# Two-layer conditioned feed-forward kernel: packed and split input loads, a reordered start of TensorE's work, and the last blocks written one tile earlier

## The reference, cut to what matters

```
W = L0_cond_weights[itok_B_0_15]                 # (128, 32, 32)
z = einsum('bct,bcd->bdt', x, W)
base = einsum('bsd,od->bso', z, W_base) + b_base
e0, e1 = z @ enc0.T, z @ enc1.T                  # ranks 32 and 8
w0, w1 = coefs0 * mask0, coefs1 * mask1          # 3 experts, (3, 512, 32) and (3, 512, 8)
decoded = einsum('bsr,eor->ebso', e0, w0) + einsum('bsr,eor->ebso', e1, w1)
update = real_fourier_orthogonal_multiply(decoded).sum(axis=0)   # fixed 512x512 orthogonal basis
x = x + base + 0.5 * update
y = einsum('bct,bcd->bdt', x, L1_cond_weights[itok_B_0_30])
x = x + scale * einsum('bsi,if->bsf', y, 2 * kernel - 1)
```

## Time and profile before

| what | before |
|---|---|
| median of three runs | 219.19 us |
| the profiled execution | 219.81 us, of which the span shown is 218.0 us |
| PE (matmul) | 213.1 us busy, 98% of the span |
| ACT | 125.2 us, 57% |
| DVE | 122.5 us, 56% |
| POOL | 111.6 us, 51% |
| one steady step of a tile on PE | 6.24 us |

### The profile page before, as it was taken

The page is one execution under the profiler, slowest core; times in us unless marked ns, Lnnn a source line. Parts: engine busy times, 40 slices in busy tenths (PEclk is TensorE's granted clock), DMA queues, the critical chain, the costliest instruction groups (busy, mean ns, idle before and its releaser), DMA issues.

```text
span 218.0 us, 4565 instructions
## 1 busy us (share of the span) xinstructions
PE 213.1 (98%) x1441; PEld 191.6 (88%) x1441; DVE 122.5 (56%) x216; ACT 125.2 (57%) x395; POOL 111.6 (51%) x133
## 2 busy tenths in 40 slices
PE   7999999999999999999999999999999999999985
PEld 2879999999999999999999999999999999999964
DVE  4676555545665554456655554566555455665443
ACT  2467765555666555556665555566655555666340
POOL 3677866655445666454446664554566645423100
PEclk9999999999999999999999999999999999999999
DMA  6991054433334444423244444333444432331112
GB/s 181 327 355 60 9 155 155 147 117 118 123 102 148 150 149 148 134 74 142 103 150 150 148 149 131 83 134 106 150 150 147 150 120 97 125 109 48 50 48 96
DMA packets 18042, 28.58 MB, mean 131 GB/s; under 512 B 3146, under 2 KB 5066, under 8 KB 18034
## 3 DMA queue, kind: packets, MB, share of 16 engines
q1 hardware_dynamic: 15360, 26.73, 36.4%
q0 software_dynamic: 2048, 1.05, 2.3%
q10 hardware_dynamic: 626, 0.70, 1.1%
HBM read 20.09 MB, written 8.39 MB: 131 GB/s over the span
## 4 chain that ended last, share of the span: by engine, by line
PE 96%; ACT 1%; DVE 1%; issue 0%
PE z_ps L565 41%; PE a_ps L608 13%; PE f_ps L619 13%; PE f_ps L615 13%; PE f_ps L597 7%; PE f_ps L600 3%; PE f_ps L512 2%; PE a_ps L518 1%; ACT blocks L311 0%; PE a_ps L619 0%; PE a_ps L615 0%; PE z_ps L512 0%; DVE a_low L465 0%; PE a_ps L546 0%; ACT a_high L347 0%
## 5 line engine op out<-in xcount | busy, mean ns | idle before, releaser
L235 POOL DMA_INDIRECT gathered<-in_L_cond_weights,row_now x56 | 54.6, 975 | 13.0 <-issue 8.9
L448 DVE TENSOR_TENSOR y_low<-a_ps,y_high 128x512 fp32r<-128x512 f32 x32 | 22.1, 692 | 67.2 <-ACT y_high L330 67.2
L330 ACT ACTIVATE y_high<-a_ps 128x512 fp32r<-128x512 f32 x32 | 19.2, 599 | 70.0 <-PE a_ps L608 70.0
L565 PE MATMUL z_ps<-a_high,xt_high 128*128 128x256 f32 x256 | 50.6, 279 | 0.2 <-DVE a_low L465 0.2
L565 PE MATMUL z_ps<-a_low,xt_high 128*128 128x256 f32 x256 | 50.4, 279 | 0.0
L242 POOL TENSOR_TENSOR x<-x_in,bias 128x512 f32<-128x512 f32 x32 | 40.9, 1280 | 14.9 <-DVE xt_low L407 11.0
L565 PE MATMUL z_ps<-a_high,xt_low 128*128 128x256 f32 x256 | 47.7, 289 | 0.0
L565 PEld LDWEIGHTS z_ps<-a_high,xt_high 128*128 128x128 f32 x256 | 41.1, 188 | 3.1 <-issue 0.5
L565 PEld LDWEIGHTS z_ps<-a_low,xt_high 128*128 128x128 f32 x256 | 38.9, 188 | 0.0
L565 PEld LDWEIGHTS z_ps<-a_high,xt_low 128*128 128x128 f32 x256 | 36.7, 190 | 0.1
L311 ACT ACTIVATE blocks<-mix_parts 32x64 fp32r<-32x64 f32 x128 | 32.6, 255 | 3.1
(11 more groups left out here) (66 smaller groups left out, 180.3 us busy)
## 6 DMA issues: line engine op xcount, KB each, us to landing
x_in<-in_x SPq DMA_DIRECT2D x32, 256.0 KB, 3.0
xt_in<-in_x_t SPq DMA_DIRECT2D x31, 256.0 KB, 2.7
out_x<-x SPq DMA_DIRECT2D x31, 256.0 KB, 2.0
gathered<-in_L_cond_weights,row_now POOLq DMA_INDIRECT x56, 2.5
w_sb<-in_L_ffn_W_base SPq DMA_DIRECT2D x3, 256.0 KB, 6.6
basis_sb<-in_fourier_basis SPq DMA_DIRECT2D x1, 258.0 KB, 3.7
w_sb<-in_L_ffn_W_base ACTq DMA_DIRECT2D x1, 256.0 KB, 6.6
xt_in<-in_x_t ACTq DMA_DIRECT2D x1, 256.0 KB
```

What stands on the lines that cost most here:

```text
L235: nc.gpsimd.indirect_dma_start(gathered[:, slot, layer, :], None, mix_rows[layer], IndirectOffsetOnAxis(rows[:, layer:layer + 1].bitcast(u ...
L448: nc.vector.tensor_tensor(out=y_low[:, slot % PAIR, :], in0=y_ps[slot % PAIR][:, :], in1=y_high[:, slot % PAIR, :].bitcast(f32), op=ALU.su ...
L565: last = nc.tensor.matmul(z_ps[slot % PAIR][:, columns], xt[:, slot % PAIR, k * P:(k + 1) * P], a[:, k, columns], start=(start and half == ...
```

## The change

It has five parts.

1. Coefficients, masks and kinds become one array `packed`, 664 words on each of 128 rows (480 of coefficients, 120 of masks, 64 of kinds). SP's queue loads rows 0 to 63 of it and of the basis, ACT's queue rows 64 to 127 (`load_side`). One semaphore for both halves.
2. SP's queue then loads W blocks 0 and 1 and both xt tiles 0 and 1, ACT's queue enc and W blocks 2 and 3.
3. 10 instead of 13 matmuls on zeros at the start, none between the transposes, and the transposes go in the order 0, 2, 1, 3.
4. `low_sum` uses all 128 rows of `enc_parts` and `spectrum_low` (which adds the product of two low parts), and follows `high_sum` bank by bank. Tile 0 is multiplied by A as its parts come (`feed0_first`), high parts first, each low part one block later.
5. In the step of tile 28, ACT and DVE also split tile 31's mix matrices, and ACT writes their blocks, after those of tile 30; the step of tile 29 has no blocks left to write.

The core of the diff:

```diff
+        def load_side(queue, rows):
+            queue.dma_start(packed[rows, :], packed_in[rows, :]).then_inc(packed_loaded, 16)
+            queue.dma_start(basis_sb[rows, :, :], basis[rows, :, :]).then_inc(basis_loaded, 16)
         def _(sp):
-            sp.dma_start(coefs_sb[:, :, :, :], coefs).then_inc(coefs_loaded, 16)
-            sp.dma_start(basis_sb[:, :, :], basis).then_inc(basis_loaded, 16)
-            for c in range(CHUNKS - 1):
-                load_w(sp, c)
+            load_side(sp, slice(0, ENC_LOW))
+            load_w(sp, 0)
+            load_w(sp, 1)
+            sp.dma_start(xt_in[:, 0, :], xt_tiles[0]).then_inc(xt_loaded[0], 16)
             sp.dma_start(xt_in[:, 1, :], xt_tiles[1]).then_inc(xt_loaded[1], 16)
         def _(act):
-            act.dma_start(masks_sb[:, :, :, :], masks).then_inc(masks_loaded, 16)
-            act.dma_start(kinds[:, :, :], kinds_in).then_inc(kinds_loaded, 16)
+            load_side(act, slice(ENC_LOW, P))
             act.wait_ge(enc_zero, 1)
             act.dma_start(enc_sb[0:R, :], enc).then_inc(enc_loaded, 16)
-            load_w(act, CHUNKS - 1)
-            act.dma_start(xt_in[:, 0, :], xt_tiles[0]).then_inc(xt_loaded[0], 16)
+            load_w(act, 2)
+            load_w(act, 3)
...
+            def feed0_first():
+                pe.wait_ge(xt_low_ready, 1)
+                for k in range(CHUNKS):
+                    pe.wait_ge(a_high_ready, k + 1)
+                    feed0_part(0, xt_high, a_high, k, start=(k == 0))
+                    feed0_part(0, xt_low, a_high, k)
+                    if k >= 1:
+                        pe.wait_ge(a_low_ready, k)
+                        feed0_part(0, xt_high, a_low, k - 1)
+                pe.wait_ge(a_low_ready, CHUNKS)
+                feed0_part(0, xt_high, a_low, CHUNKS - 1, stop=True).then_inc(fed0, 1)
...
```

More of the change, by code:

```diff
@@ L358, in _, with step @@
             expand0(1, 1)
-            def step(tile, u, turn, early=False, new=True):
+            def step(tile, u, turn, early=False, last=False, new=True):
                 high_y(tile, u, recycled=not early or u >= PAIR)
-                split_mix((u + 2) % RING, turn + (u + 2) // RING)
+                if new:
+                    split_mix((u + 2) % RING, turn + (u + 2) // RING)
+                if last:
+                    split_mix((u + 3) % RING, turn + (u + 3) // RING)
                 if new:
@@ L365, in step @@
                 high_z(tile + 2, (u + 2) % RING)
-                expand1((u + 2) % RING, tile + 2, recycled=not early or u >= 2)
-                expand0((u + 2) % RING, tile + 2)
+                if new:
+                    expand1((u + 2) % RING, tile + 2, recycled=not early or u >= 2)
+                    expand0((u + 2) % RING, tile + 2)
+                if last:
+                    expand1((u + 3) % RING, tile + 3)
+                    expand0((u + 3) % RING, tile + 3)
             for u in range(RING):
@@ L373, in _ @@
                     step(turn * RING + u, u, turn)
-            step(TILES - 4, 0, TURNS - 1)
+            step(TILES - 4, 0, TURNS - 1, last=True)
             step(TILES - 3, 1, TURNS - 1, new=False)
@@ L476, in _, with step @@
             dve.wait_ge(scale_loaded, 16)
-            def step(tile, u, early=False):
+            def step(tile, u, early=False, last=False):
                 low_y(tile, u, recycled=not early or u >= PAIR)
                 low_mix(tile + 2, (u + 2) % RING)
+                if last:
+                    low_mix(tile + 3, (u + 3) % RING)
                 low_xt(tile + 3, (u + 3) % RING)
@@ L657, in _ @@
                 feed1(TILES - 1, 3, end_ps[half], halves[half])
-INPUTS = ["x", "x_t", "kinds", "L0_cond_weights", "L0_ffn_W_base", "L0_ffn_b_base", "enc", "coefs", "masks",
+INPUTS = ["x", "x_t", "packed", "L0_cond_weights", "L0_ffn_W_base", "L0_ffn_b_base", "enc",
           "L1_cond_weights", "L1_ffn_kernel", "L1_ffn_scale"]
@@ L681 @@
     inputs["x_t"] = np.asarray(inputs["x"]).reshape(TILES, P, CHUNKS, P).transpose(0, 3, 2, 1).reshape(TILES, P, T)
-    inputs["kinds"] = kinds_by_partition(inputs["itok_B_0_15"], inputs["itok_B_0_30"])
+    kinds = kinds_by_partition(inputs["itok_B_0_15"], inputs["itok_B_0_30"])
     inputs["enc"] = np.concatenate([inputs["L0_ffn_enc0"], inputs["L0_ffn_enc1"]])
-    inputs["coefs"] = by_partition(inputs["L0_ffn_coefs0"], inputs["L0_ffn_coefs1"])
-    inputs["masks"] = by_partition(inputs["L0_ffn_mask0"], inputs["L0_ffn_mask1"])
+    parts = (by_partition(inputs["L0_ffn_coefs0"], inputs["L0_ffn_coefs1"]),
+             by_partition(inputs["L0_ffn_mask0"], inputs["L0_ffn_mask1"]), kinds)
+    inputs["packed"] = np.concatenate([np.ascontiguousarray(part).reshape(P, -1).view(np.int32) for part in parts], axis=1)
     arrays = {name: np.ascontiguousarray(inputs[name]) for name in INPUTS}
```

58 lines of the change are left out of this document (24 added, 34 removed).

## The result

| | before | after |
|---|---|---|
| median (range) of six runs each, us | 219.15 (218.78 to 219.70) | 217.76 (217.55 to 218.38) |
| ratio, 95% interval | | 0.9934 [0.9915, 0.9953] |
| profiled execution, its span | 219.81, 218.0 | 217.55, 215.7 |

The change makes the kernel 1.4 us faster, inside the range given (215.5 to 218.0) and 1.2 us short of the 216.6 forecast. Span against span it is 2.3 us, near the 2.55 of the sum. The two differ because single executions scatter: 18 of the kernel before on another chip took 218.67 to 220.79. Its profiled one lay 0.66 above the median here, and the changed kernel's profiled one was the fastest of its six. What was slow in the first is worked out further down, under *The base*.

A forecast was written before the change was run, and what follows sets the result against it. PE, 96% of the span, bounds the kernel and only its two ends can pay: 1.6 us (start) plus 0.95 (end) takes 219.81 to 217.3; with the median 0.6 lower, the forecast is 216.6, range 215.5 to 218.0.

The forecast's parts named there:

- the sum: Whole kernel: 1.6 us from the start plus 0.95 from the end, 2.55 in all, off the profiled execution.
- The base: Starting point of the sum: the profiled execution of 219.81 us, with the median taken as 0.6 lower, at 219.19.
- Part 5: End, tile 31: PE's wait of 0.79 us for ACT's blocks goes; gain 0.95 us (0.8 to 1.1).
- Part 4: Start, ACT: waits for tile 0's second gather until 14.6, then 5.5 us; `mix1` at 20.1, 1.6 us earlier, not 2.6.
- Part 1: Start: basis matmuls begin at 6.25 instead of 6.47, gain 0.2 us (0 to 0.5); packed load costed at nothing.
- Part 2: Transposes and sums: fillers between transposes go, saving 0.88 us; bank 0 complete 1.65 earlier, `a_high` at 10.65.
- Rows cost nothing: Low sums: 128 rows instead of 64 take no longer, three sums 0.89 against 0.87 us, row-count changes included.
- Part 3: Tile 0's feed: only two matmuls follow the last `a_low`; tile 1's feed starts at 14.15 instead of 16.73, 2.6 earlier.
- Rival (a): Start: the gathers land sooner, so the gain is 3.55 us, time 215.6; chance 0.17.
- Rival (b): Start: TensorE's clock rises only after the basis matmuls, which take 1.8 us longer; time 217.4; chance 0.14.
- Rival (c): Start: the packed load lands 1 us later, gain 0.6 + 0.95, time 217.6; chance 0.09 together with another rival.
- Rival (d): Start: clock stays at 1.2 GHz up to tile 0's feed; 3.2 us slower, 222.4; chance 0.05.

The follow-up runs named there:

- change, again: The changed kernel unaltered, run once more beside its variants on one chip: ratio 0.9928 to the kernel before, 218.16 us.
- 13 fillers: The changed kernel with 13 instead of 10 matmuls on zeros at the start: ratio 0.9922 to the kernel before, 218.00 us.
- loads as before: The changed kernel with parts 1 and 2 undone (separate loads, old queues), W transposed in order 0, 1, 3, 2: ratio 0.9892 to before, 217.14 us.
- the same, gathers ahead: Kernel of the row above, x tiles 1-3 and xt 3 issued after tile 0's matrices landed: 0.9857 (loads as before), 0.9851 (whole pieces), 0.9897 (basis whole).
- gathers ahead: The changed kernel with SP issuing x tiles 1 to 3 and xt tile 3 only after tile 0's matrices landed: ratio 0.9909 to before, 217.50 us.
- whole pieces: The changed kernel with packed loaded whole on SP's queue and the basis whole on ACT's queue: ratio 0.9907 to before, 217.79 us.
- basis whole: The changed kernel with the basis in one piece on SP's queue, packed still in halves: ratio 0.9915 to before, 217.84 us.
- no fillers: The variant with loads as before and gathers ahead, without any matmul on zeros at the start: ratio 0.9892 to the kernel before, 217.55 us.
- low sums on 64 rows: The variant with loads as before and gathers ahead, its low sums back on 64 rows: ratio 0.9908 to the kernel before, 217.86 us.
- the new end alone: The kernel before with only tile 31's mix matrices split and its blocks written in tile 28's step: ratio 0.9956 to the kernel before.

## Why the prediction was right in kind and short in size

The start obeys two marks. `mix1` of tile 0 starts at the later of: first `a_high` plus 9.0 us (PE's and ACT's own work), and the start of ACT's split of tile 0's matrices plus 5.6 us (where ACT had waited for them).

| kernel | first a_high | split of matrices | mix1 | by a_high + 9.0 | by split + 5.6 |
|---|---|---|---|---|---|
| change | 11.66 | 15.04 | 20.61 | 20.66 | 20.64 |
| change, again | 12.32 | 15.20 | 21.14 | 21.32 | 20.80 |
| 13 fillers | 11.26 | 15.12 | 20.70 | 20.26 | 20.72 |
| loads as before | 11.22 | 14.56 | 20.23 | 20.22 | 20.16 |
| the same, gathers ahead | 10.16 | 13.27 | 19.17 | 19.16 | 18.87 |
| gathers ahead | 11.96 | 14.41 | 20.97 | 20.96 | no wait |
| whole pieces | 10.48 | 15.26 | 20.84 | 19.48 | 20.86 |
| the same, gathers ahead | 10.55 | 13.00 | 19.56 | 19.55 | no wait |
| basis whole | 12.43 | 15.24 | 21.25 | 21.43 | 20.84 |
| the same, gathers ahead | 11.21 | 13.98 | 20.22 | 20.21 | 19.58 |
| no fillers | 12.05 | 14.50 | 21.06 | 21.05 | no wait |
| low sums on 64 rows | 11.07 | 14.60 | 21.23 | 20.07 | no wait |

The whole pieces with gathers ahead were forecast by this rule before they ran. The two kernels with slow basis matmuls come 0.18 under it. The last row lies outside it: there the sums themselves take longer, so `a_high` is no longer followed by the same work. The expectation of the whole pieces with gathers ahead says "in every profile" and overlooks that row.

Of the 1.2 us by which the forecast was too low, about half comes from the base it was taken from, and half from the start, where `mix1` came at 20.61 and not at 20.1.

Point by point:

- *Part 5* was forecast at 0.95 and gave 1.05 in the profile and 1.0 by itself. Right.
- *Part 4*, that the gather is what comes late next, was right in mechanism: forecast 5.5 us from its landing to `mix1`, measured 5.6. The term was mis-sized at its start: the landing was taken as unchanged at 14.6 and came at 15.0, for the second gather took 6.9 us instead of 6.2. In the other two profiles of the change's loads with the SP queue untouched it was 15.2 and 15.1.
- *Part 1* is the step of the start that failed. "I cost the load at nothing" looked at the packed load alone, and bounded that; the basis half and enc on ACT's queue, which the same edit moved, were not priced at all. enc stood behind 92 KB on that queue before and behind 295 KB now. In the first profile they put the basis matmuls at 6.84 instead of 6.25 and `spectrum_low` half a us later still. The basis mark is not steady: it was 6.20, 6.24 and 6.41 in the three other profiles with these loads. Steady in all four is that ACT's half of the basis landed 1.1 to 1.9 us behind SP's, and that ACT split enc at 6.97 to 7.56, against 5.01 to 5.74 in the ten others. Undoing parts 1 and 2 gives 0.8 to 1.0 us back. Halving takes part in this: with gathers ahead in both, halves stand at 0.9909 [0.9878, 0.9940] and whole pieces at 0.9851 [0.9832, 0.9870]. The two profiles differ most in W's blocks, which whole pieces let the queues issue 0.8 to 1.2 us sooner: PE waited 0.84 us for them with halves, not at all with whole pieces. The Trainium skill (DMA: Bandwidth & Descriptors, Rules for kernel authors) advises against two transfers to disjoint partition halves; these runs agree, and say that it is worse than useless here.
- *Part 2* forecast `a_high` at 10.65, measured 11.66: 0.6 of the miss from the basis, 0.3 from the wait for W's last block, the rest mostly from `spectrum_low`, which was late with enc. Costing W's waits "at nothing" was too little: weight loads or matmuls of PE waited for W blocks in 8 of the 14 profiles, by 0.2 to 0.8 us in six and by 1.3 and 1.4 us in two. "Rows cost nothing" holds for rows (three sums in 0.87 or 0.89 us) but not for a change of rows, and the slip was in favour of the change: in the new order low sums on 64 rows would have cost 1.1 us.
- *Part 3* said that `a_low` would be the late one. It was ready at 14.77, and PE's feed of tile 1 began at 15.59: PE is still the late one, for its eight sums and 24 feeds take 10.72 to 15.59 without a gap. The forecast had 9.80 to 14.15, half a us too little. It did not cost much, the gather being nearly as late.
- *Rival (a)*, gathers sooner, did not occur, but can be made: one wait on SP does it. *Rival (b)*, the late clock, did occur: in three profiles (the change again, the basis whole, no fillers) the basis matmuls ran at 1.2 GHz throughout. In the change `mix1` came 0.5 us later for it (21.14 against 20.61), not 0.8: the slow matmuls took 1.7 us more, but the basis had landed 0.64 sooner and no W block was late. *Rival (c)* was half right: the basis was what two queues made late; `packed` was late by 0.3 us at the median of the profiles, halved or whole, so not by its halving. *Rival (d)* did not occur: no run shows the clock falling over sixteen transposes in a row. They ran at 0.10 to 0.12 each in all profiles where no W block was waited for, and the sums behind them at the full clock.
- *The base* is the other step that failed. The profiled execution of 219.81 had a slow start. Its 13 matmuls on zeros ran at the low clock nearly to the end, 0.41 us apart (1.20 to 6.47), and held the basis matmuls back to 6.47, though `decode` was ready at 5.95. The kernel with the new end alone has the same start, and in its profile the last four of them started some 0.27 us apart (4.67 to 5.74), for the clock had risen:

```profile
4.67 1.03 PE L520 MATMUL f_ps<-idle 128*128 128x512 bf16 x4
5.74 0.49 PE L534 MATMUL z_ps<-basis_sb,decode 128*128 128x129 f32 x2
...
21.01 1.16 PE L616 MATMUL a_ps<-blocks,x 128*128 128x128 f32 x8
```

  Here `mix1` comes at 21.01 instead of 21.73, 0.5 us of it by the clock and 0.3 by an earlier `decode`. So the gain "21.73 to 20.1" already held most of what made that execution slow, and "the median lies 0.6 below" took it off a second time. Without that step the forecast is 217.3; with `mix1` 0.5 later and the end 0.1 better than in the sum it is 217.7, and 217.76 was measured. This account fits the numbers but is not proven: how the start of before is spread over its executions is known from these two profiles only. By the ratios, part 5 gives 0.44%, parts 3 and 4 on the old loads another 0.64% (0.9956 to 0.9892), and parts 1 and 2 take 0.36% back (0.9892 to 0.9928). That is 1.0 + 1.4 - 0.8 = 1.6 us, with 0.4 to 0.5 us of doubt on each ratio.

Left open: why ACT's half of the basis is later than SP's. Both were issued at 1.36; ACT's issue took 0.85 us, SP's 0.58; the same queue carried the whole basis in 3.9 us when it stood first. That W's first block on SP's queue overtakes it fits, but was not tried by itself. Open too is whether the gain of whole pieces lies in the basis, in enc or in W's earlier issue, for they moved together.

## What to carry to other kernels

Price every load behind the one that an edit touches, on its queue, down to the first reader; a threshold over two queues waits for the slower. When a start is sped up on the busiest engine, look for the longest chain that does not go through that engine: here it ran from the first load over an index computation to an indirect DMA, and it ate up what faster loads gave (whole pieces, `mix1` at 20.84) until loads that nobody needed yet were issued after it (19.56). Judge such a change by marks in several profiles, since two single profiles here disagreed with twelve timed runs by 0.9 us. And ask of the execution that a sum starts from whether its own start was a slow one, before carrying the sum to the median.

## What the runs showed of the hardware that was not expected

- An indirect DMA's time to landing depends on what other queues are given beside and behind it: the second gather took 6.9 us with four 256 KB loads issued around it and 5.8 us without them; over all profiles 6.2 to 7.0 us against 4.3 to 5.8.
- Two halves of 129 KB, issued together from two queues, landed after 3.4 to 3.5 us on SP's queue and after 4.6 to 5.3 us on ACT's, in four profiles. A half of 64 rows also took longer to issue: 0.56 to 0.58 us as the first DMA of its queue, where a piece of 128 rows took 0.39 to 0.41.
- The same kernel's start has TensorE at full clock by the tenth matmul on zeros in one profile, and only after the eight basis matmuls (9.8 us) in another. These then cost 3.6 instead of 1.9 us, though the clock row of the profile's page reads full throughout.
- Alternating matmuls of 64 and 128 rows start 0.43 us apart at 512 columns, against 0.23 without the change of rows.
